# Values' term of the output product on 32x32 tiles, write product by chunk at its chain step, T in eighths, and a new order of the program

## The reference, cut to what matters

```python
x = x + 0.5 * ffn(layernorm(x), ...)          # token shift, r = sigmoid, k = relu^2
x = x + attn(layernorm(x), ...)
x = x + 0.5 * ffn(layernorm(x), ...)

def step(S, inp):                              # attn, token by token, per head
    qt, kt, vt, gt, bt = inp
    S = S * jnp.exp(gt)[..., None, None]
    pred = jnp.einsum('bhk,bhkv->bhv', kt, S)
    dv = (vt - pred) * bt[..., None]
    S = S + jnp.einsum('bhk,bhv->bhkv', kt, dv)
    ot = jnp.einsum('bhk,bhkv->bhv', qt, S)
    return (S, ot)
```

## Time and profile before

| what | value |
|---|---|
| median of 3 runs | 1807.67 us (1795.96 to 1810.2) |
| profiled execution, own time | 1813.92 us |
| its span | 1812.1 us |
| PE busy | 1715.9 us (95%), 45056 matmul records |
| DVE busy | 1299.3 us (72%) |
| ACT busy | 1054.2 us (58%) |
| POOL busy | 474.5 us (26%) |

### The profile page before, as it was taken

How to read it: one execution, slowest core, us unless ns; L and a number is a source line. 1 busy time by engine, 2 the same in 40 slices (tenths; PEclk the granted TensorE clock), 3 DMA queues, 4 the chain that set the end, 5 groups by cost and what they waited for, 6 DMA issues and landing times.

```text
span 1812.1 us, 100548 instructions
## 1 busy us (share of the span) xinstructions
PE 1715.9 (95%) x45056; PEld 1457.9 (80%) x45056; DVE 1299.3 (72%) x3718; ACT 1054.2 (58%) x2157; POOL 474.5 (26%) x389
## 2 busy tenths in 40 slices
PE   5799999999999999999999999999999999999986
PEld 3588888888888888888888888888888888888775
DVE  3777777787777777777778777777877777877531
ACT  4556656665666655566566566565656556655432
POOL 0223332222333221333222133322123323212201
PEclk9899999999999999999999999999999999999766
DMA  3000000000000000000000000000000000000000
GB/s 117 1 4 4 16 15 4 15 15 15 16 15 15 4 15 15 16 15 16 4 16 15 15 16 15 15 4 15 15 15 15 16 4 9 10 9 10 10 9 12
DMA packets 21582, 26.42 MB, mean 15 GB/s; under 512 B 2209, under 2 KB 20769, under 8 KB 21153
## 3 DMA queue, kind: packets, MB, share of 16 engines
q1 hardware_dynamic: 21152, 19.99, 3.4%
HBM read 11.60 MB, written 8.39 MB: 11 GB/s over the span
## 4 chain that ended last, share of the span: by engine, by line
PE 83%; issue 9%; DVE 5%; ACT 1%; POOL 1%; DVEq 0%; POOLq 0%; ACTq 0%
PE ps L241 38%; PE ps L223 16%; PE ps L232 10%; PE ps L216 6%; PE ps L454 3%; PE ps L209 2%; PE ps L404 2%; PE ps L552 2%; PE ps L352 2%; PE ps L544 2%; PE ps L370 1%; DVE XK L1060 1%; DVE XR L1301 1%; DVE SA L1105 1%; DVE KD L1343 1%
## 5 line engine op out<-in xcount | busy, mean ns | idle before, releaser
L241 PE MATMUL ps<-MQ,S 64*64 64x16 f32 x4096 | 255.3, 211 | 0.6 <-ACT S L621 0.6
L241 PE MATMUL ps<-WP,V 64*64 64x16 f32 x4096 | 252.9, 210 | 0.0
L241 PEld LDWEIGHTS ps<-MQ,S 64*64 64x64 f32 x4096 | 213.5, 140 | 45.7 <-issue 44.0
L1073 DVE SCALAR_TENSOR_TENSOR CV<-ps,cw,CV 128x256 f32<-128x256 f32 x576 | 233.8, 476 | 7.0 <-ACT CV L670 7.0
L241 PEld LDWEIGHTS ps<-WP,V 64*64 64x64 f32 x4096 | 214.4, 141 | 0.0
L999 POOL COPY TZ<-t_one 128x512 f32<-128x512 f32 x32 | 19.5, 609 | 727.0 <-DVE T L1111 727.0
L241 PEld LDWEIGHTS ps<-SA,MQ 32*32 32x32 f32 x8192 | 92.2, 109 | 72.1 <-issue 37.6
L241 PE MATMUL ps<-KQI,K 64*64 64x48 f32 x4096 | 138.7, 222 | 4.1 <-issue 3.8
L241 PE MATMUL ps<-SA,MQ 32*32 32x16 f32 x8192 | 117.3, 182 | 26.0 <-DVE SA L1105 20.7
L223 PE MATMUL ps<-w_r_ffn,XR 128*128 128x256 f32 x512 | 133.8, 406 | 2.3 <-DVE XR L1060 2.3
L216 PE MATMUL ps<-XK,w_k_ffn 128*128 128x256 f32 x512 | 128.5, 396 | 7.8 <-DVE XK L1060 7.8
(11 more groups left out here) (138 smaller groups left out, 3835.7 us busy)
## 6 DMA issues: line engine op xcount, KB each, us to landing
X<-in_x SPq DMA_DIRECT2D x32, 256.0 KB, 2.9
out_x<-X SPq DMA_DIRECT2D x32, 256.0 KB, 2.3
KQI<-in_blocks SPq DMA_DIRECT2D x2, 256.0 KB, 4.2
w_r_ffn<-in_wT_r_ffn SPq DMA_DIRECT2D x1, 256.0 KB, 3.3
w_k_ffn<-in_wT_k_ffn SPq DMA_DIRECT2D x1, 256.0 KB, 3.6
w_v_ffn<-in_wT_v_ffn SPq DMA_DIRECT2D x1, 256.0 KB, 4.5
w_k<-in_wT_k SPq DMA_DIRECT2D x1, 256.0 KB, 4.5
w_q<-in_wT_q SPq DMA_DIRECT2D x1, 256.0 KB, 4.7
```

What stands on the lines that cost most here:

```text
L241: last = mm(ps[rows, o:o + n], stat[rows, pk].rearrange("p s c -> p (s c)"), mov[rows], **flags)
L1073: stt(d4[:, m], src, cw[:, i, m, tap:tap + 1], d4[:, m], ALU.mult, ALU.add).then_inc(signal, 1)
```

## The change

The values' term of `o_product` uses V2 with 2 slots instead of V4 with 4, and so 32x32 tiles; in each call the four packs of the states' term come first and the four of the values' term after them, with `start` on the first pack alone. `b_product` makes one chunk per call (eight calls), each placed before the chain step of that chunk, and now also waits for the copy of the chunk before. `t_product` has eight calls of 4 packs; the first ends a step and the others begin the next one. `v_slots` makes 2 copies instead of 4. All four order lists, the table of banks and the waits that follow from it are new; ScalarE sets a table six times per step instead of twice.

```diff
-PS = {"xt1": 5, "yt": 4, "xt3": 1, "r1": 2, "k1": 5, "v1": 6, ...
+PS = {"xt1": 5, "yt": 1, "xt3": 5, "r1": 1, "k1": 4, "v1": 2, ...
...
-        K4, KD4, V4, S4 = (sb(n, [P, PACKS, HT, C]) for n in ("K4", "KD4", "V4", "S4"))
+        K4, KD4, S4 = (sb(n, [P, PACKS, HT, C]) for n in ("K4", "KD4", "S4"))
+        V2 = sb("V2", [P, PACKS, 2, C])
...
-                bk = (PS["t0"], PS["t0"], PS["t1"], PS["t1"])[q]
-                for pk in range(q * RING, (q + 1) * RING):
+                bk = PS["t0"] if q < 4 else PS["t1"]
+                for pk in range(q * RING // 2, (q + 1) * RING // 2):
...
-            def b_product(g, q):
-                if q == 0:
+            def b_product(g, n):
+                if n == 0:
                     pe.wait_ge(s["wp"], 2 * g + 2)
                     pe.wait_ge(s["vt"], g + 1)
-                if g and q == 0:
-                    pe.wait_ge(s["ch_s"], 8 * g)
+                if g or n:
+                    pe.wait_ge(s["ch_s"], NCH * g + n)
...
             def turn3(g):
                 pe.wait_ge(s["xn3"], g + 1)
                 if g < GROUPS - 3:
-                    pe.wait_ge(s["cq"], 6 * g + 24)
-                    pe.wait_ge(s["tapq"], g + 4)
+                    pe.wait_ge(s["cv"], 6 * g + 24)
+                    pe.wait_ge(s["tapv"], g + 4)
...
-                for pk in range(h * PACKS // 8, (h + 1) * PACKS // 8):
-                    o = PS["o"] * BANK + pk * C
-                    pairs(o, C, S4, pk, MQ[g % 2][:, pk, U:], start=True, stop=False)
-                    last = pairs(o, C, V4, pk, WP[g % 2][:, pk, U:], start=False, stop=True)
+                part = range(h * PACKS // 8, (h + 1) * PACKS // 8)
+                for pk in part:
+                    pairs(PS["o"] * BANK + pk * C, C, S4, pk, MQ[g % 2][:, pk, U:], start=(pk == 0), stop=False,
+                          skip_group_check=True)
+                for pk in part:
+                    last = pairs(PS["o"] * BANK + pk * C, C, V2, pk, WP[g % 2][:, pk, U:], start=False, stop=True,
+                                 skip_group_check=True)
                 last.then_inc(s["o_ps"], 1)
...
-                in_slots(V4, VT[g % NVT][:], s["v_slots"])
+                in_slots(V2, VT[g % NVT][:], s["v_slots"])
```

More of the change, by code:

```diff
@@ L371, in q_proj @@
                 last.then_inc(s["q_ps"], 1)
[L373 to L374 removed]
+            def b_product(g, n):
+                if n == 0:
                     pe.wait_ge(s["wp"], 2 * g + 2)
                     pe.wait_ge(s["vt"], g + 1)
[L377 to L378 removed]
+                if g or n:
+                    pe.wait_ge(s["ch_s"], NCH * g + n)
                 w2 = WP[g % 2][:, :, 0:U].rearrange("p k (s c) -> p k s c", s=2)
[L380 to L384 removed]
+                for ub in range(M * B):
+                    pk = ub * NCH + n
+                    last = pairs(PS["b"] * BANK + (n * M * B + ub) * D, D, w2, pk, VT[g % NVT][:, pk * C:(pk + 1) * C],
+                                 start=(n == 0 and ub == 0), stop=False, skip_group_check=True)
                 last.then_inc(s["b_ps"], 1)
@@ new lines, in _ @@
+                on(tap_v, step - 1)
+                on(v_slots, step - 3)
+                on(halo3, step - 4)
+                on(relu1, step)
+                on(s_slots, step - 3)
+                on(xt3, step - 4)
+                silu_set()
+                on(gate, step - 1)
+                on(silu_q, step - 1)
+                on(tanh1, step)
+                on(square_k, step - 1)
+                ln_exp_set()
+                on(rstd2, step)
+                on(gates_wide, step - 1)
@@ L941, in _ @@
+                on(halo_y, step)
+                on(norm2, step)
         @block.gpsimd
@@ L1428, in _ @@
                 on(solve_sub, step - 3, 12)
[L1429 to L1439 removed]
+                on(mix_r3, step - 5)
@@ L1440, in _ @@
+                on(solve_mul, step - 3, 13)
+                on(solve_sub, step - 3, 13)
+                on(soft_max, step - 2)
+                on(gates, step - 2)
+                on(solve_mul, step - 3, 14)
+                on(shift2, step - 1)
+                on(solve_sub, step - 3, 14)
+                on(t_turn, step - 3)
+                on(stats1, step)
                 on(k_normed, step - 2)
-                on(o_norm, step - 4)
                 on(d_out0, step - 3)
+                on(shift1, step)
@@ L1451, in _ @@
                 on(mix_k1, step)
+                on(chain, step - 3, 1)
+                on(stats3, step - 4)
+                on(mix_r1, step)
+                on(gram0, step - 2)
+                on(gram1, step - 2)
+                on(gram2, step - 2)
+                on(chain, step - 3, 2)
+                on(gram3, step - 2)
                 on(shift3, step - 4)
-                on(x3, step - 5)
-                on(chain, step - 3, 0)
-                on(conv_q, step - 1)
                 on(gates_in, step - 1)
-                on(chain, step - 3, 1)
```

385 lines of the change are left out of this document (174 added, 211 removed).

## The result

The changed kernel takes 1763.07 us (median of four runs, 1762.18 to 1768.82) against 1808.93 of the kernel before, run beside it: ratio 0.9759, with a 95% interval of 0.9719 to 0.9799. That is 2.4% faster, where 0.9% was forecast. In the profiled executions the span fell from 1812.1 to 1760.8 us, by 51.3. The range held the time by one microsecond at its lower end. The size of the gain is that of rival 4, which had said that nearly all waits go and had given no reason for it.

The account below looks back on a forecast made before the run. PE's work plus about 1.1 us of waiting per step bound it. Work 0.63 less, chain waits 0.2 less, issue waits 0.3 more: 0.5 to 0.6 less per step, placed at -17 us, forecast 1791 us, range 1762 to 1828.

Parts of the forecast that it names:

- rival 4: Whole step: all waits but 0.3 us go, 1.4 us per step, 44 us less, about 1764 us; chance 0.16.
- PE's own work: Sum of PE's pieces: output product 0.43, write product and chain 0.2, grams 0.2, less 0.2 for borders; 0.63 us per step less.
- unit prices: PE times read from start distances: output call 0.94 us, write-and-chain pair 0.66, leaving a small tile size 0.07 to 0.14.
- Rival 1, the full drain: Tile-size borders: each costs a full drain of 0.2 us, 1.4 us lost per step, about 1830 us; chance 0.05.
- Waits on the chain: PE waiting for VectorE: 0.3 us per step after, where 0.5 was, with DVE 0.1 to 0.7 late at `turn3`.
- Instruction stream: PE's "issue" waits: from 0.64 to 0.94 us per step, bounded by 0.64 and 1.9.
- Rivals 3 and 5: 3: VectorE's list binds, 1830 us, chance 0.08; 5: borders and waits return the gain, within 6 us of 1808, 0.20.
- The ends: Pipeline fill and empty: about one uncovered ScalarE table load in each of some five steps, 5 to 6 us, between 0 and 20.
- rival 2: Instruction stream binds: "issue" goes from 0.64 to 2.9 us per step, step 1.6 longer net, about 1840 us; chance 0.07.

Follow-up runs that it names:

- the fourth experiment: The changed kernel with T's eighths 1 to 7 in one row, and the transpose, decay sums and output squares behind them: 1856.09 us, ratio 1.0244.
- the sixth: The kernel before with the write product in eight calls, each directly ahead of its chain step, all other work unmoved: 1900.52 us, ratio 1.0533.
- the last: The kernel before with the key squares between output product and T, and the first block's r and v products apart: 1837.65 us, ratio 1.0209.
- the eighth: The changed kernel with the output product in four pieces, sixteen packs of each term apart between 128-row blocks: 1785.19 us, ratio 0.9892.
- the staggered terms: The changed kernel with the output product in four pieces that overlap the two terms, in groups of 12, 10 and 10 packs: 1754.33 us, ratio 0.9712.
- The third: The kernel before with the v projection moved between chain steps 5 and 6: 1859.13 us, ratio 1.0292.
- twelfth: The kernel before with the v projection between chain steps 5 and 6 and the third block's r product ahead of the output product: 1839.86 us, ratio 1.0177.
- thirteenth: The twelfth's kernel with a 128-row block after every two calls of the output product: 1804.63 us, ratio 1.0005.
- the fifth: The changed kernel with the output product's two terms alternating at every pack, 64 changes of tile size instead of 16: 2121.77 us, single execution.

## Why the prediction was right in sign and too small

*PE's own work: right.* Forecast 0.63 us per step less. The unit prices came out to a hundredth, 0.94 for a call and 0.66 for a pair; a block of 128 takes 3.90 where two of 64 took 2.00 each, so the border between was worth 0.10 instead of 0.14. Summed over all neighbouring pieces of PE by their undisturbed distances in the two traces, a step has 51.5 us of work before and 50.8 to 50.9 after, some 0.7 less.

*Rival 1, the full drain: wrong.* A border costs 0.11 where it was tried 64 times per step, about half of a record's 211 ns, and 0.08 to 0.11 in the changed kernel. (The prediction's "under half a record" fits its 0.07 to 0.08; its 0.14 was two thirds of one.) The Trainium skill, "TensorEngine Tiling (Array Packing)", section Key Properties, says that a change of mode drains the engine; these runs show no wait for all of a record's time.

*Waits on the chain: right in mechanism, a little too high.* Forecast 0.3 us per step with DVE 0.1 to 0.7 late for `turn3`; it is 0.18, at that place. One part was not seen: by distances of starts the stall between chain steps 5 and 6 is 0.51 us beyond the usual, where the wait row shows 0.36, and that at `turn3` is 0.24. The gain is 0.27 where 0.2 was forecast.

*Instruction stream: the step that failed.* The prediction took 0.94 us per step for "issue" after the change and bounded it by 0.64 and 1.9. It is 0.27, below the lower bound. The view counts idle time only, and leaves out part of each stop. By distances of starts, all stops of over 0.15 us from 400 to 1550 us, other than the stall between chain steps 5 and 6 and that at `turn3`, are 28.1 us before and 11.2 after, 1.30 and 0.50 per step. So the stream gave 0.8 where the prediction had it take 0.3. That is 1.1 of the 1.2 us by which the step came out shorter than forecast. With 0.27 of the chain and 0.7 of work it makes the 1.74 measured.

What failed in it is that the rate was formed over a whole step: 9% more instructions, a third more fast records. What decides is where they stand. A packet of the q8 queue is 16 KB, and between two packets PE takes about 256 instructions. Two stops of the trace of before:

```profile
889.76 0.70 PE L241 MATMUL ps<-GK,T 32*32 32x32 f32 x58
891.12 0.26 PE L241 MATMUL ps<-GK,T 32*32 32x32 f32 x6 [0.66 <-issue]
...
996.20 0.40 PE L241 MATMUL ps<-GK,T 32*32 32x32 f32 x25
997.55 0.54 PE L241 MATMUL ps<-GK,T 32*32 32x32 f32 x39 [0.95 <-issue]
```

For the first a packet starts at 888.42 us; PE's last start is at 890.27, and it goes on at 891.12. For the second a packet starts at 995.11; PE stops at 996.41 and goes on at 997.55. For the stop inside gram, one starts at 911.50; PE stops at 913.23 and goes on at 913.89. So PE goes on 2.4 to 2.7 us after the packet's start each time. Nor are these three chosen ones: of the 35 stops over 0.3 us outside the chain steps, from 400 to 1550 us, 32 end 2.0 to 3.0 us after the start of a packet, where about a quarter of all PE's starts lie so; in the changed kernel it is 10 of 10. If what PE has in hand runs out before the packet is there, it stands. In the three stops it had issued 116 to 200 instructions since the packet's start. Those last long where 128-row records of 0.23 us are among them, and short where 32x32 records of 9.2 ns follow a run of their own kind. Outside T, the d products and the grams, the new order puts a slow block of 1.9 us behind nearly every 0.66 or 1.9 us of small products; the old one had a T of 64, d of 64, T of 64 and pairs of b and gram in close neighbourhood. The one-way tests are the fourth experiment (same instructions, closer: waits x5, in one long execution), the sixth (closer: x3), the last (farther: x0.55), and the eighth (longer runs of 32x32: x3). They show that placement sets these waits; how many fast records in a row can be borne they don't fix, as the staggered terms show.

The Trainium skill, "Runtime: NRT & Kernel Launch", section Instruction fetch mechanics, calls the cost of such fetches mostly hidden. In the changed kernel this nearly holds (0.5% of the stretch is spent so); in the kernel before it is 1.2%, and in the sixth experiment 3.6%.

*Rivals 3 and 5* did not occur. DVE is just hidden, as counted. *The ends* cost some 3 us; 5 to 6 were taken for them. *Small slips* that touch no result: the clock is below 9 in the last three slices of the earlier trace rows, not four, and three rivals' times were added up too low. By the prediction's own steps rival 1 is 40 us over before, 1848 and not 1830; rival 2 is 1.6 per step, 1857 and not 1840; rival 3 is 0.9 per step, 1836 and not 1830.

*Which move of the order is worth how much stays open.* Three single edits of the old order were each slower (1.0292, 1.0533, 1.0209). Only the sixth experiment's is a part of the change as it stands. The third puts a block between chain steps 5 and 6, where the new order has another one, and the last puts one between output product and T, where the new order has none. With two further moves the third came to 1.0005. The gain was not split further: 1.58 of the 1.74 us belong to the new order with the write product by chunk and T in eighths. That the clock's stretches follow from rows of small products without slow blocks between is shown for the old order (twelfth against thirteenth); for the fourth and sixth kernels it is only read from where they stand, and there PE also stood still for "issue" ahead of most falls, so that idle time isn't excluded.

## What to carry to other kernels

In a kernel that is bound by one engine in order, add up distances of starts, borders included, and then ask of each new neighbourhood how many instructions go by in the 2 to 3 us between a packet's start and PE's going on: totals per step say nothing of that. Split a term onto smaller tiles only where slow blocks can stand between the rows of fast records; here the split alone lost 1.3%, and the rest of the change without it gained 1.9%. Before an instruction is moved, name what it has been covering: of the three single edits of the old order two uncovered waits for other engines, 13.1 and 24.1 us in 1150, that were dearer than what they removed.

## What the runs showed of the hardware

The clock can fall behind a run of small-tile records though PE has no gap. In the twelfth experiment PE is busy 4.00 of 4.00 us with records of 16 columns ahead of the fall to 0.50, and in the fifth, whose product is all such records with a border after every few, the mean clock is 0.85. With a 128-row block after every two calls, in the thirteenth, it fell once. The share of busy time gave no warning: PE is 100% busy ahead of the fall.

Waits that go with instruction fetch can be longer than those for any engine: 41.2 us in 1150 in the sixth experiment, in stops of up to 2.0 us, with the same count of instructions as the kernel before (100548), which has 14.3. The engine with the most there is VectorE, 7.4 by its chain copy.
